# Attention's products taken two and two: two scores, then two row maxima, in each half step

## The reference, cut to what matters

```python
x = x + attention(layernorm(x))          # q, k, v with biases; q also gets ocr_bias
scores = q @ k.T / sqrt(32) + band       # band: 0.1 where |i - j| <= 2
attn = softmax(scores, axis=-1); out = attn @ v; out @ Wo.T + bo
x = x + linear(layernorm(x))             # inputs and weights rounded to an FP6 grid in blocks of 32
```

## Time and profile before

| | |
|---|---|
| median of 3 runs | 4168.13 us (4163.34 to 4171.36) |
| the profiled execution | 4178.3 us |
| its span | 4176.5 us, 59567 instructions |
| mean granted clock of TensorE | 0.989 |

### The profile page before, as it was taken

One profiled execution on the slowest core, in us unless ns is written; L12 is line 12 of the kernel. 1 busy time (PEld: TensorE's weight loads), 2 busy tenths in 40 slices (PEclk: granted clock), 3 DMA queues, 4 the chain that ended last, 5 costly groups with the idle time before them and its releaser, 6 DMA issues.

```text
span 4176.5 us, 59567 instructions
## 1 busy us (share of the span) xinstructions
PE 4036.3 (97%) x21328; PEld 2538.5 (61%) x21328; DVE 3359.0 (80%) x5630; ACT 2408.2 (58%) x4651; POOL 3034.4 (73%) x1118
## 2 busy tenths in 40 slices
PE   8999999999999999999999999999999999977998
PEld 6788875555555555555555555555555555536787
DVE  6444568888888888898888888888888888846886
ACT  2222216766667666766676677676676767652332
POOL 2111008888989888988888888988888888964552
PEclk9999999999999999999999999999999999988999
DMA  7888859999999999999999999998999899876664
GB/s 245 266 261 264 235 151 183 187 205 195 196 198 194 204 187 208 188 206 186 209 192 195 197 196 200 196 203 181 207 184 209 180 214 191 199 169 169 180 172 101
DMA packets 292270, 825.16 MB, mean 198 GB/s; under 512 B 28832, under 2 KB 95392, under 8 KB 229536
## 3 DMA queue, kind: packets, MB, share of 16 engines
q0 software_dynamic: 72960, 486.57, 59.2%
q1 hardware_dynamic: 219040, 335.09, 28.6%
HBM read 211.82 MB, written 156.24 MB: 88 GB/s over the span
## 4 chain that ended last, share of the span: by engine, by line
PE 77%; DVE 14%; ACT 4%; DMA 4%; issue 1%; SPq 0%; POOL 0%; POOLq 0%; ACTq 0%; DVEq 0%
PE ps_a L862 20%; PE ps_a L848 20%; PE ps_b L827 17%; PE ps_p L481 12%; DVE part_max L1039 8%; PE ps_b L893 3%; ACT p_sb L1015 3%; DVE p_sb L1066 2%; PE ps_b L940 2%; PE ps_b L873 1%; DMA o_first<-o_d 1%; DMA q_st<-shift 1%; PE ps_a L923 1%; DMA q_lo_d<-s_lo 0%; PE ps_t L499 0%
## 5 line engine op out<-in xcount | busy, mean ns | idle before, releaser
L1039 DVE TENSOR_REDUCE part_max<-ps_b 128x1 f32<-128x512 f32 x4016 | 2465.1, 678 | 379.4 <-PE ps_b L827 379.1
L1205 POOL TENSOR_TENSOR pair<-p_sb 128x2048 f32<-128x2048 f32 x512 | 2454.9, 4815 | 78.0 <-ACT p_sb L1015 59.3
L1015 ACT ACTIVATE p_sb<-ps_a 128x512 f32<-128x512 f32 x4096 | 2084.1, 614 | 726.0 <-PE ps_a L848 721.8
L862 PE MATMUL ps_a<-p_sb,v_sb 128*32 128x512 f32 x8192 | 993.5, 602 | 38.7 <-DVE p_sb L1066 23.0
L848 PE MATMUL ps_a<-q_st,k_odd 97*128 97x512 f32 x2048 | 845.2, 415 | 18.2 <-ACT p_sb L1015 17.8
L848 PE MATMUL ps_a<-q_st,k_even 97*128 97x512 f32 x2048 | 845.6, 413 | 7.5 <-PEq L163 3.8
L827 PE MATMUL ps_b<-k_odd,q_st 96*128 96x512 f32 x2048 | 813.6, 397 | 0.0
L827 PE MATMUL ps_b<-k_even,q_st 96*128 96x512 f32 x1968 | 783.4, 398 | 0.0
L848 PEld LDWEIGHTS ps_a<-q_st,k_odd 97*128 97x128 f32 x2048 | 388.0, 190 | 344.6 <-issue 214.6
L848 PEld LDWEIGHTS ps_a<-q_st,k_even 97*128 97x128 f32 x2048 | 388.2, 190 | 324.1 <-issue 218.5
L862 PEld LDWEIGHTS ps_a<-p_sb,v_sb 128*32 128x32 f32 x8192 | 224.1, 109 | 522.6 <-ACT p_sb L1015 321.5
(11 more groups left out here) (111 smaller groups left out, 2859.6 us busy)
## 6 DMA issues: line engine op xcount, KB each, us to landing
pair<-pair POOLq DMA_DIRECT2D x448, 1024.0 KB, 8.9
q_st<-q_hi_d SPq DMA_DIRECT2D x128, 256.0 KB, 7.2
xin<-in_x SPq DMA_DIRECT2D x16, 1024.0 KB, 8.7
xb_d<-xb SPq DMA_DIRECT2D x16, 1024.0 KB, 5.9
q_hi_d<-s_hi SPq DMA_DIRECT2D x64, 256.0 KB, 6.3
q_lo_d<-s_lo SPq DMA_DIRECT2D x64, 256.0 KB, 7.3
k_hi_d<-s_hi SPq DMA_DIRECT2D x64, 256.0 KB, 3.6
k_lo_d<-s_lo SPq DMA_DIRECT2D x64, 256.0 KB, 4.4
```

The source lines that it names most:

```text
L862: last = nc.tensor.matmul(ps_a[h * HD:(h + 1) * HD, RING_S, :], v_sb[:, kt, h * HD:(h + 1) * HD], p_sb[:, s % SLOTS, h, :], start=(kt == 0 ...
L1015: nc.scalar.activation(p_sb[:, s % SLOTS, h, :], ps_s[:, (HG * s + h) % RING_S, :], ACT.Exp, scale=SCALE).then_inc(p_ready, 1)
L1039: nc.vector.tensor_reduce(part_max[:, unit % 2, col, n:n + 1], ps_m[:, max_place(unit, j) % RING_M, :], AX.X, ALU.max).then_inc(max_taken, 1)
L1205: nc.gpsimd.tensor_tensor(pair[:, m % PAIR_RING], p_sb[:, s % SLOTS], p_sb[:, (s + 1) % SLOTS], ALU.add).then_inc(paired, 1)
```

## The change

It reorders two kinds of instruction in TensorE's queue. In a half step (heads 0 and 1, or 2 and 3) the order was score, maximum product, score, maximum product; it becomes score, score, maximum product, maximum product. The burst keeps its place before head 2 of the odd steps, and `between_scores` (pieces of the first output projection, in the last unit) is called once in a half step, with the odd head, the only one for which it did anything. No other queue is touched, no instruction is added or removed, and every wait keeps its value.

```diff
             for s in range(ST + 2):
-                for h in range(HG):
-                    if s % 2 == 1 and h == HG // 2:
+                for heads in ((0, 1), (2, 3)):
+                    if s % 2 == 1 and HG // 2 in heads:
                         burst(s)
                     if s < ST:
-                        score(s, h)
-                        ahead(*max_at(s, h))
+                        for h in heads:
+                            score(s, h)
+                        for h in heads:
+                            ahead(*max_at(s, h))
                         if s >= ST - KT:
-                            between_scores(s % KT, h)
+                            between_scores(s % KT, heads[1])
```

## The result

The changed kernel took 4234.36 us in the median of 4 runs (4223.41 to 4244.35), against 4165.74 us (4162.36 to 4171.36) for the one before on the same chip: 1.0152 times, 95% interval 1.0138 to 1.0167. The forecast was 4234 us. The profiled execution took 4233.52 us, its span 4231.7, which is 55.2 over the span of before.

A forecast was written before the change was run, and what follows sets the result against it. The prediction took TensorE's queue as the bound. Odd scores 46, periods behind a copy 6 and bands 14 us summed to 66 us, making 4234 us on the median of 4168.13, with a range from 4186 to 4270.

The forecast's parts named there:

- The bound: Whole kernel: TensorE's queue sets the time, busy for 97% of the span.
- Odd scores: Periods without a full band: S7's late load makes each 0.12 us longer, 384 x 0.12 = 46 us.
- E4: Fifth of a period's eight exponentials on ScalarE: ends at +3.12, unmoved by earlier scores, and releases the load of S7.
- The smaller gap of 216 ns: Same-kind neighbours on TensorE: if they fell from 230 to 235 ns to 216, the sum would be 58 us.
- Periods behind a copy: Periods where ScalarE copies first: E4 ends some 0.05 us later, about 126 periods, 6 us.
- S7: Last of a period's eight scores: its load waits for E4 until +3.17, so it starts 0.12 us late.
- Even maximum products: VectorE's takes start 0.235 us later; hidden by S7's delay with 0.10 to spare, otherwise costing 0.02.
- Bands: Periods with full bands: bands and burst come 0.11 us later, between 0.08 and 0.235; 128 x 0.11 = 14 us.
- The sum: Whole kernel: 46 + 6 + 14 = 66 us, giving 4234 us on the median, 1.6% slower.
- the rival that made this the outcome: Longer periods let GpSimd's additions end before the bands, removing waits: faster, 4136 us; chance 0.06.
- A hidden late load: Score loads on TensorE: a late load costs nothing, no measurable change, 4176 or 4168 us; chance 0.07.
- VectorE as the bound in every period: Late takes drag maximum products in every period and the bands: 120 us, 4288 us; chance 0.08.

The follow-up runs named there:

- The last pair alone: Against the kernel before, only the pair before the burst reordered (two scores, then their two maximum products), other pairs alternating: 4219.81 us, 1.0135.
- the short exponentials: Exponentials of 448 of 512 columns, against the kernel before: 4203.32 us, 1.0089 in the changed order; 4166.38 us, 0.9997 in the old order.
- the kernel with three pairs: Against the kernel before, all pairs reordered but the one before the burst: 4222.69 us, 1.0133.
- the first pair alone: Against the kernel before, only the first pair behind the burst reordered (two scores, then their two maximum products): 4198.80 us, 1.0078.
- the order with two maxima first: Against the kernel before, two maximum products and then two scores in every half step: 4212.29 us, 1.0106.
- the kernels without bands: The band of the mask left out, against the kernel before: 4358.79 us, 1.0466 in the changed order; 4273.50 us, 1.0254 in the old order.

## Why the prediction was right

**The bound.** That TensorE's queue sets the time held in the plain periods: what the change cost came as waits in it. In periods with full bands VectorE's round of 6.05 us sets the time, which the prediction had as 6.0 but used only to size its term for bands.

**Odd scores, 46 us.** Right in place, cause and size. The loads at +1.18, +2.19 and +3.17, the unmoved end of E4 and a period of 5.92 are the forecast's numbers. The last pair alone and the short exponentials show the cause. The value taken for a late load, 0.10 us between 0 and 0.19, decided the size: 0.12 us a plain period predicted, 0.13 measured. It was a choice by the nearest row, and a good one. That the three delays don't add was right too, and the kernel with three pairs shows it. The smaller gap of 216 ns for neighbours of one kind, from which the prediction drew its 58 us, didn't come: in the changed kernel a score starts 0.236 us behind the score before it, in the median.

**Periods behind a copy, 6 us.** Right. From burst to burst, the median period with the copy of the sums went from 6.67 to 6.85 and the one with the copy of the output from 5.80 to 5.99: 0.18 and 0.19, where 0.12 + 0.05 was worked out. Only the second is clean: the period with the sums also grows to 6.81 when the first pair alone is reordered and S7 isn't late.

**Even maximum products, hidden.** Right in the full change, where 18.6 us of waits for takes are listed against 14.7. Alone, without S7's delay to cover it, the part costs 32 us (second kernel) and 37 (4203.32 - 4166.38, short exponentials). The prediction put that case at 0.02 a period, which holds for plain periods, and missed that bands, the turned row and the reciprocal each make it dearer. Some of it shows through in the full change too. The 16 periods with the reciprocal grew by 0.23 (5.99 to 6.22), and so did 32 of those with full bands: 16 that also have the sums (6.85 to 7.09) and 16 of the fourth block of queries (6.05 to 6.28). All three kinds grew as much with the first pair alone, and next to nothing with the last pair alone. Over what S7's late load costs the other periods, that is some 4 us in all.

**Bands, 14 us.** This is the term that was too large. The median period with full bands and nothing else went from 6.02 to 6.10, which is the 0.08 of the term's lower end. The 127 periods with full bands between the first burst and the last, 796.5 us in all, take 803.2 in the changed kernel: 7 us more, half of the term. I had leaned to the row at hand, whose band was held by GpSimd.

**The sum.** From the first burst to the last the profiled executions differ by 57.8 us: 6.7 in those periods, and 51.1 in the other 384, where 46 + 6 = 52 was predicted. The clock moves these a little. Eight periods of before touch stretches at the 1.2 GHz level and are together 32 us longer than the median of their kind; in the changed kernel it is six periods and 27 us. Without these excesses the other periods grew by 55.7 us and those with bands by 7.8, together 63 where 66 was forecast.

**What came back.** The page shows less waiting for GpSimd: the band instructions took 209.1 us for 223.5 on the page of before. Of the 352, 153 began during an addition of GpSimd in the kernel before, and 38 in the changed one. Every one of them ended only after that addition. So the rival that made this the outcome had the right mechanism. But VectorE gained these 14 us and TensorE little of them: where the second block of queries has its bands, the period that weighs the third pair of steps went from a mean of 6.41 to 6.23, but that of the fourth from 6.61 to 6.64. What came back for certain is no more than the 3 us of the first; how much in all isn't shown. The medians of the runs differ by 69 us, the ratio gives 63; with runs that spread over 20 us, a forecast of 4234 for a median of 4234 is in part luck.

**The rivals.** A hidden late load is refuted by the last pair alone. VectorE as the bound in every period is refuted by the order with two maxima first, which has the same loss with the takes early. The Trainium skill, page "SBUF — State Buffer", section "Who interferes with whom", has a VectorE instruction with two SBUF inputs and a GpSimd one that reads SBUF exclude each other by a lock; the traces agree, since no band instruction of either kernel ended within an addition that it had begun in.

## What to carry to other kernels

In a queue that never seems to wait, look at how far each load of weights starts behind the matmul before it: a load that is held while its matmul isn't shows the slack, here 0.1 us in 5.8. Whether a reordering spends it is told by two distances: how far apart the products will stand in TensorE's queue, and how far apart the engine that empties their banks finishes (0.48 us for an exponential). Count from the first to the last product of a kind between two points that nothing passes, not product by product, and expect parts that share slack not to add. An order moves where a bound shows and need not take it away. Less work for the engine behind it can bring out another wait, as in the kernels without bands.

## What was not expected of the hardware

Less work for VectorE made the kernel slower: without its bands, the row of maxima (8 KB) landed 6.2 us behind its issue, not 3.5, nearly every unit began with a wait, and behind nearly half of these waits the clock fell. What the row most likely waits for can be read from the traces. It leaves on SP's queue, and a transfer of 1 MB from GpSimd's queue is under way. The issues of both, and the first score, without bands in the old order, and then the issues in the kernel before:

```profile
1166.14 0.87 POOL L1210 DMA_DIRECT2D pair<-pair  x1 [0.56 <-POOL pair L1205]
1167.30 0.51 SPq L682 DMA_DIRECT2D q_st<-shift  x1
...
1173.24 0.50 PE L848 MATMUL ps_a<-q_st,k_even 97*128 97x512 f32 x1 [1.10 <-DMA q_st<-shift]
```

```profile
1148.66 0.86 POOL L1210 DMA_DIRECT2D pair<-pair  x1 [0.55 <-POOL pair L1205]
1153.92 0.52 SPq L682 DMA_DIRECT2D q_st<-shift  x1
```

In the first the transfer takes 7.2 us and the row 5.9, so that they land at 1173.3 and 1173.2; in the second 7.4 and 2.3, landing at 1156.1 and 1156.2. This holds for most units: the row lands within 0.5 us of the transfer issued last before it in 51 of 63 units of before and in 47 of 63 without bands. In before that transfer leaves 4.7 us ahead of the row, in the median, and is mostly done; without bands it leaves 1.15 us ahead. No run moved that transfer alone, so that it holds the row up is inferred from these times.

What a late load costs can be read in the period above. The loads of S3, S5 and S7 start 0.15, 0.20 and 0.17 us behind the starts of S2, S4 and S6 (2122.21, 2123.17, 2124.18). The matmul two places behind those starts at 2122.70, 2123.72 and 2124.69, 0.49, 0.55 and 0.51 later, where 0.47 is two free places: the delays are 0.02, 0.08 and 0.04. The whole stretch from 720 to 3700 us agrees (S3, S5 and S7 of every period at the full clock, medians): a load 0.15 us behind the start of the score before it gives 0.489 us to the start of the maximum product behind both, 0.20 gives 0.541, and 0.24 gives 0.580. So here a load may be about 0.13 us late at no cost, a figure that is drawn back from these, and every bit beyond that is paid in full. The Trainium skill, page "TensorE: Matmul & The Clock Gate", section "The mechanism", lists that a load overlaps a running matmul only where their groups of array rows differ, though the text above that list names the background weight buffer as a second way; here a load of 97 rows at 2123.37 runs under a matmul of 97 rows that started at 2123.17 and is booked for 0.4 us, in the same rows. The measurement decides against the list.
